# Key sums in one transfer a unit, powers per four units, Sign for ternary weights, half the key squares on GpSimd, and a new order at the end of the feed-forward

## The reference

```python
x = x + tanh(g_xattn[0]) * L0_xattn(ctx, layernorm(x))   # state-space block over ctx, gated by silu of the norm
x = x + tanh(g_ffn[0])   * L0_ffn(layernorm(x))          # gated feed-forward, weights made ternary, activations to 8 bits
x = x + tanh(g_xattn[1]) * L1_xattn(layernorm(x), ctx)   # attention, 16 heads of 128, RMS norm on q and k
x = x + tanh(g_ffn[1])   * L1_ffn(layernorm(x))          # four experts, token i goes to expert i % 4
...
gamma_w = clip(mean(abs(w)), 1e-05)
w_dq = clip(round(w / gamma_w), -1, 1) * gamma_w         # so a weight is -1, 0 or 1 times gamma_w
...
k = rmsnorm((ctx @ Wk).reshape(B, Skv, H, D), gk)        # k * (mean(k*k) + eps) ** -0.5 * gk
```

## Time and profile before

| what | value |
|---|---|
| median of 3 runs (lowest, highest) | 1853.01 us (1847.89, 1858.5) |
| the profiled execution's own time | 1852.26 us |
| its span in the profile | 1850.5 us |
| busy: PE, DVE, ACT, POOL | 1763.2, 1300.1, 963.8, 666.5 us |
| granted TensorE clock, mean | 0.983 of full speed |
| first attention step on PE | at 385.93 us |

### The profile page before, as it was taken

One profiled execution on the slowest core, in us unless ns is written; L12 is line 12 of the kernel. 1 busy time (PEld: TensorE's weight loads), 2 busy tenths in 40 slices (PEclk: granted clock), 3 DMA queues, 4 the chain that ended last, 5 costly groups with the idle time before them and its releaser, 6 DMA issues.

```text
span 1850.5 us, 19507 instructions
## 1 busy us (share of the span) xinstructions
PE 1763.2 (95%) x6114; PEld 809.9 (44%) x6114; DVE 1300.1 (70%) x1899; ACT 963.8 (52%) x1920; POOL 666.5 (36%) x696
## 2 busy tenths in 40 slices
PE   8999899879999999999999999999999899999999
PEld 4333344334444444444444444444444344445543
DVE  4989686989998689899787998987652444422221
ACT  7988786446545546566455566555435334320100
POOL 2434322337463324557222564562223333310000
PEclk9999899979999999999999999999999999999999
DMA  7999833767851146897212589732112799837110
GB/s 262 242 289 286 244 109 116 203 164 187 199 142 57 51 100 162 208 240 200 66 30 74 156 188 251 199 95 69 35 57 91 218 282 293 236 119 273 40 51 28
DMA packets 159045, 292.11 MB, mean 158 GB/s; under 512 B 18424, under 2 KB 51704, under 8 KB 156000
## 3 DMA queue, kind: packets, MB, share of 16 engines
q1 hardware_dynamic: 141664, 227.95, 39.0%
q0 software_dynamic: 17280, 62.92, 17.5%
HBM read 169.51 MB, written 58.26 MB: 123 GB/s over the span
## 4 chain that ended last, share of the span: by engine, by line
PE 72%; DVE 13%; ACT 6%; issue 4%; DMA 3%; POOL 1%; SPq 1%; DVEq 0%; ACTq 0%; POOLq 0%
PE p L846 11%; PE p L806 10%; PE p L823 9%; PE p L857 8%; PE p L893 6%; PE p L697 5%; DVE s_M L1025 5%; PE p L780 4%; PE p L829 4%; PE p L908 3%; PE p L746 3%; PE p L785 3%; DVE s_M L1020 2%; DVE s_M L1032 1%; DVE s_U L1178 1%
## 5 line engine op out<-in xcount | busy, mean ns | idle before, releaser
L1025 DVE TENSOR_TENSOR_SCAN s_M<-s_M 128x1024 f32<-128x1024 f32 x128 | 296.4, 2315 | 9.9 <-ACT s_M L1290 7.6
L1178 DVE CUSTOM_DVE_ANT_0 s_U<-p,s_U 128x512 f32<-128x512 f32 x256 | 188.2, 745 | 161.0 <-PE p L823 159.7
L823 PE MATMUL p<-s_U 128*128 128x512 f32 x512 | 268.2, 612 | 4.6 <-DVE s_U L1178 3.0
L806 PE MATMUL p<-s_U 128*128 128x512 f32 x512 | 256.7, 610 | 3.4 <-ACT s_U L1418 2.7
L1534 POOL DMA_DIRECT2D s_u<-s_M x120 | 111.7, 931 | 383.7 <-DVE s_M L1032 355.6
L1579 POOL TENSOR_SCALAR s_U<-s_U 128x512 f32<-128x512 f32 x256 | 231.9, 926 | 6.3
L857 PE MATMUL p<-s_U 128*128 128x512 f32 x512 | 223.7, 593 | 0.0
L846 PE MATMUL p<-s_U 128*128 128x512 f32 x472 | 216.0, 599 | 2.5 <-ACT s_U L1431 2.4
L1431 ACT COPY s_U<-p 128x512 f32<-128x512 f32 x196 | 105.5, 594 | 176.3 <-PE p L829 175.0
L1290 ACT ACTIVATE s_M<-s_dl,s_small 128x511 f32<-128x511 f32 x256 | 170.3, 717 | 35.5 <-DVE s_M L1025 35.3
L1426 ACT ACTIVATE s_U<-s_U 128x512 f32<-128x512 f32 x256 | 181.6, 710 | 5.3
(11 more groups left out here) (194 smaller groups left out, 2458.3 us busy)
## 6 DMA issues: line engine op xcount, KB each, us to landing
s_u<-s_M POOLq DMA_DIRECT2D x120, 512.0 KB, 7.6
s_bc<-bc_scratch SPq DMA_DIRECT2D x96, 256.0 KB, 4.5
k_scratch<-s_U SPq DMA_DIRECT2D x16, 1024.0 KB, 7.9
v_scratch<-s_U SPq DMA_DIRECT2D x16, 1024.0 KB, 5.4
s_U<-in_Wq SPq DMA_DIRECT2D x64, 256.0 KB, 6.6
s_U<-k_scratch SPq DMA_DIRECT2D x64, 256.0 KB, 5.4
s_U<-rk_scratch SPq DMA_DIRECT2D x64, 256.0 KB, 5.8
s_U<-in_Wo SPq DMA_DIRECT2D x64, 256.0 KB, 4.5
```

The costliest lines, as they stand in the source:

```text
L806: ins = e.matmul(banks[bk][:], wqq[j % 2][:, k, :], axT[b % 2][:, k, :], start=(k == 0), stop=(k == 3))
L823: e.matmul(banks[bk][:], qT[j % 3][:, k * 128:(k + 1) * 128], kT[j % 2], start=True, stop=True).then_inc(S["a_s"], 1)
L1025: e.tensor_tensor_scan(w, dA[i % 2], w, 0.0, ALU.mult, ALU.add).then_inc(S["m_s"], 1)
L1178: e.tensor_tensor_reduce(out=Pm[j % 2][:, k, :], in0=banks[ABANK[kind, j, k]][:], in1=rkb[j % 2], scale=rq[:, k:k + 1], scalar=-3.0e38, op ...
```

## The change

1. **Key sums.** `nv` writes to one of two tiles `ksr[n % 2]`. `r` is one transfer of four rows of 2 KB to a new scratch `rs_scratch`. After the second key product of the next group of four units, `ld` waits for all four and loads 128 x 64 numbers to `krs`; four `pw` of 16 columns follow after that unit's key products, and one `st` stores 128 x 64 numbers in the next unit. `rk_scratch` is laid out by group, so the first heads of the attention wait for the first group alone. The store of the keys and the load of `Wk` are issued one and two steps earlier (at `k` 3), `r` ahead of `v` 3.
2. **Key squares.** Products 0 and 2 of a unit are squared by POOL from the copy in SBUF (new instruction, a `tensor_tensor` of 128x512), 1 and 3 by ACT as before. `n` waits for both engines. The PSUM bank of an even product is given back after its copy.
3. **Ternary weights.** `clip` is gone: `put` is `Sign(x - MAGIC)` on ACT, with a bias tile `down` that POOL sets.
4. **End of the feed-forward.** In `ffn_order()` the steps `l` of a tile stand at other places among the products of the next, and `st`, `hn`, `xt` are steps of F: those of tiles 0 to 2 stand before the last residual, those of tile 3 after it. The separate list `XT` is gone.
5. The planner's tables follow, so the order changes on all engines.

```diff
-        QUANT += [("clip", w, c)] if c < 4 else []
...
-            order += [("m", t, 2 * c)] + (leave[:1] if c == 0 else []) + [("m", t, 2 * c + 1)] + (leave[3:] if c == 2 else leave[c + 1:c + 2] if c < 2 else [])
-            if c:
-                order += enter[:1]
-                enter = enter[1:]
-        order += enter
+            order += [("m", t, 2 * c)] + (leave[:1], leave[1:3], leave[3:4], enter[2:])[c]
+            order += (enter[:1] if c == 1 else []) + [("m", t, 2 * c + 1)] + (leave[4:] + enter[1:2] if c == 2 else [])
         leave = [("l", t, k) for k in range(5)]
-    return order + leave
+    order += leave[:1] + [("st", t, 0) for t in range(3)] + leave[1:4] + [("hn", t, 0) for t in range(3)] + [("xt", t, 0) for t in range(3)]
+    return order + leave[4:] + [("st", 3, 0), ("hn", 3, 0), ("xt", 3, 0)]
...
+        first, second = q > 0 and b == 0, q > 0 and b == 1
+        KV += [(b, q, "k", 0), (b, q, "k", 1)] + ([(NB - 1, q - 1, "ld", 0)] if first else []) + [(b, q, "k", 2), (b, q, "k", 3)]
+        KV += [(NB - 1, q - 1, "pw", i) for i in range(4)] if first else []
+        KV += [(b, q, "v", 0), (b, q, "v", 1), (b, q, "n", 0)] + ([(NB - 1, q - 1, "st", 0)] if second else [])
+        KV += [(b, q, "v", 2), (b, q, "nv", 0), (b, q, "r", 0), (b, q, "v", 3)]
+KV += [(NB - 1, 3, "ld", 0)] + [(NB - 1, 3, "pw", i) for i in range(4)] + [(NB - 1, 3, "st", 0)]
...
-                        e.wait_ge(S["k_sq"], 4 * n + 4)
+                        e.wait_ge(S["k_sq"], 2 * n + 2)
+                        e.wait_ge(S["k_sp"], 2 * n + 2)
...
-                        e.activation(dst, stg[c], ACT.Copy, bias=-MAGIC, saturate=False).then_inc(S["q_put"], 1)
+                        e.activation(dst, stg[c], ACT.Sign, bias=down[:], saturate=False).then_inc(S["q_put"], 1)
...
-                        e.activation(ksq[i], banks[bk][:], ACT.Square).then_inc(S["k_sq"], 1)
+                        if i % 2:
+                            e.activation(ksq[i], banks[bk][:], ACT.Square).then_inc(S["k_sq"], 1)
...
-                        if n:
-                            e.wait_ge(S["d_ksr"], 64 * n)
-                        e.activation(ksr, banks[bk][:], ACT.Copy, bias=EPS, scale=1.0 / HD).then_inc(S["k_nv"], 1)
+                        elif n:
+                            e.wait_ge(S[f"d_ksr{n % 2}"], 16 * (n // 2))
+                        e.activation(ksr[n % 2], banks[bk][:], ACT.Copy, bias=EPS, scale=1.0 / HD).then_inc(S["k_nv"], 1)
...
+                        e.tensor_tensor(ksq[i], ks[2 * n % NKS][:, i, :], ks[2 * n % NKS][:, i, :], ALU.mult).then_inc(S["k_sp"], 1)
+                    elif kind == "pw":
+                        power(krs[:, 64 * q + 16 * i:64 * q + 16 * i + 16], (S["d_kr"], 16 * (q + 1)), "k_p")
...
+                        e.dma_start(rsd[16 * q + 4 * b:16 * q + 4 * b + 4], ksr[n % 2][0:128:32, :]).then_inc(S[f"d_ksr{n % 2}"], 16)
+                    elif kind == "ld":
+                        e.wait_ge(S["d_ksr0"], 32 * (q + 1))
+                        e.wait_ge(S["d_ksr1"], 32 * (q + 1))
+                        e.dma_start(krs[:, 64 * q:64 * q + 64], rsd[16 * q:16 * q + 16].rearrange("r (p c) -> (r p) c", c=64)).then_inc(S["d_kr"], 16)
                     elif kind == "st":
-                        e.wait_ge(S["k_p"], n + 1)
-                        e.dma_start(rkd[j:j + 4].rearrange("h (p c) -> (h p) c", c=16), krs[:, 16 * n:16 * n + 16]).then_inc(S["d_rk"], 16)
+                        e.wait_ge(S["k_p"], 4 * (q + 1))
+                        e.dma_start(rkd[16 * q:16 * q + 16].rearrange("r (p c) -> (r p) c", c=64), krs[:, 64 * q:64 * q + 64]).then_inc(S["d_rk"], 16)
```

More of the change, by code:

```diff
@@ L112, in silu @@
     return b == 0 and t < 2
-XT = [("st", t) for t in range(4)] + [("hn", t) for t in range(4)] + [("xt", t) for t in range(4)]
 LBANK = {}
@@ L132 @@
             names += [("o", t)]
-    names += [("xt", t) for t in range(4)]
+        elif kind == "xt":
+            names += [("xt", t)]
     for i, x in enumerate(names):
@@ L139 @@
     for b in range(NB):
-        last = ((b - 1) % NB, q - (b == 0))
-        KV += [(b, q, "k", i) for i in range(4)] + [(b, q, "v", 0), (b, q, "v", 1), (b, q, "n", 0), (b, q, "v", 2), (b, q, "nv", 0)]
-        KV += [(*last, "pw", 0)] if q or b else []
-        KV += [(b, q, "v", 3), (b, q, "r", 0)] + ([(*last, "st", 0)] if q or b else [])
-KV += [(NB - 1, 3, "pw", 0), (NB - 1, 3, "st", 0)]
+        first, second = q > 0 and b == 0, q > 0 and b == 1
[4 more added lines that the diff above has]
+KV += [(NB - 1, 3, "ld", 0)] + [(NB - 1, 3, "pw", i) for i in range(4)] + [(NB - 1, 3, "st", 0)]
 KBANK = {}
@@ L299, in forward @@
             part(name, [("POOL", 1.3)], ("e", t, 1))
+        elif kind == "st":
+            part(("xst", t), [("DVE", 1.0), ("POOL", 1.0)], ("l", t, 4))
+        elif kind == "hn":
+            part(("xhn", t), [("DVE", 0.6)], ("xst", t), ("l", 3, 0))
+        elif kind == "xt":
+            part(("xxt", t), [("PE", 0.6), ("ACT", 0.7)], ("xhn", t), *([(NB, "q", NH * (b - 1) - 1, 3)] if b > 1 else []), take=[("xt", t)], free=[("xt", t)])
         elif k == 0:
@@ L308, in forward @@
             part(name, [("DVE", 0.8)], ("l", t, 3), ("o", t, 0), free=[("o", t)])
-    for kind, t in XT:
-        if kind == "st":
-            part(("xst", t), [("DVE", 1.0), ("POOL", 1.0)], ("l", t, 4))
-        elif kind == "hn":
-            part(("xhn", t), [("DVE", 0.6)], ("xst", t))
-        else:
-            part(("xxt", t), [("PE", 0.6), ("ACT", 0.7)], ("xhn", t), *([(NB, "q", NH * (b - 1) - 1, 3)] if b > 1 else []), take=[("xt", t)], free=[("xt", t)])
     return out
@@ L328, in weights @@
             out.append(("Q", [("ACT", 2.0)], [(0, "thr", w, 0)], (0, kind, w, c), [], []))
-        elif kind == "clip":
-            out.append(("Q", [("DVE", 1.3)], [(0, "rnd", w, c)], (0, kind, w, c), [], []))
         elif kind == "put":
-            out.append(("Q", [("ACT", 2.0)], [(0, "clip", w, c)], (0, kind, w, c), [], []))
+            out.append(("Q", [("ACT", 2.0)], [(0, "rnd", w, c)], (0, kind, w, c), [], []))
         else:
@@ L344, in keys @@
         does = {"k": [("PE", 1.75), ("ACT", 1.2)], "v": [("PE", 1.75), ("ACT", 0.6)], "n": [("PE", 1.2)], "nv": [("ACT", 0.6)],
-                "r": [("DMA", 5.0)], "pw": [("POOL", 3.0)], "st": [("DMA", 8.0 if (b, q) == (NB - 1, 3) else 2.5)]}[kind]
-        needs = {"nv": [("K", at.get((b, q, "n", 0)))], "n": [("K", at.get((b, q, "k", 3)))], "r": [("K", at.get((b, q, "nv", 0))), ("K", n - 1)], "pw": [("K", at.get((b, q, "r", 0))), ("K", n - 1)], "st": [("K", at.get((b, q, "pw", 0))), ("K", n - 1)]}.get(kind, [])
+                "r": [("DMA", 2.0)], "ld": [("DMA", 3.0)], "pw": [("POOL", 4.0)], "st": [("DMA", 8.0 if q == 3 else 2.5)]}[kind]
+        if kind == "k" and i % 2 == 0:
+            does = [("PE", 1.75), ("ACT", 0.6), ("POOL", 1.5)]
+        needs = {"nv": [("K", at.get((b, q, "n", 0)))], "n": [("K", at.get((b, q, "k", 3)))], "r": [("K", at.get((b, q, "nv", 0))), ("K", n - 1)], "ld": [("K", at.get((b, q, "r", 0))), ("K", n - 1)], "pw": [("K", at.get((b, q, "ld", 0)))], "st": [("K", at.get((b, q, "pw", 3))), ("K", n - 1)]}.get(kind, [])
         take = [bank] if kind in "kvn" else []
@@ L541, in flamingo @@
         ks = [U[:, 15360 + 2048 * i:17408 + 2048 * i].rearrange("p (h t) -> p h t", h=4) for i in range(NKS)]
-        ksr = U[:, 26624:27136]
+        ksr = [U[:, o:o + 512] for o in (26624, 25600)]
         ksq = [U[:, 21504 + 512 * i:22016 + 512 * i] for i in range(4)]
```

102 lines of the change are left out of this document (44 added, 58 removed).

## The result

The changed kernel takes **1891.9 us** (median of 4 runs, 1885.8 to 1897.5) against 1852.0 of the kernel before (4 runs on the same chip): a ratio of **1.0217, 95% interval 1.0194 to 1.024**. So it is slower beyond the noise; whether by 2% or more, the interval leaves open. The prediction was 1842 us with a range up to 1863. The profiled execution, 1897.5 us, was the longest of the four, so the two traces lie 45 us apart where the medians lie 40.

A forecast was written before the change was run, and what follows sets the result against it. The prediction took PE's work to bound the kernel, leaving only its idle and low-clock time to gain. Its terms, -9 - 11 - 4 - 2 + 8 + 3 + 2 + 5 - 2 = -10 us, gave 1842 us, range 1823 to 1863.

The forecast's parts named there:

- POOL's line: At three group borders, column sums wait for squares on POOL behind its powers and transfers: +8, +3, +2 us.
- the key sums: Before 245 us, two tiles and one transfer remove PE's 6.6 us wait and its low clock: -9 us (-3 to -9.6).
- the clips: Twelve clips, 14.6 us, leave DVE in M0; no PE wait names them, so 0 on PE.
- what lies behind the first step: After the attention's start, DVE further in M1 and new ends of F1 to F3: -2 us (-10 to +5).
- The prediction's own sign of being wrong: PE's idle time up to the attention stays at 36 us or grows, or the gain is lost between 386 and 600 us.
- End of F0, -11 and -4: Ready K work fills PE's 12.8 us idle at F0's end: -11 us; less low clock behind those waits: -4 us.
- Squares, -2: ACT loses 32 squares up to the attention, shortening PE's other waits for `nv`: -2 us (0 to -4.2).
- Rival D: Little changes: full DMA queues set the pace up to 245 us, attention starts cold; about 1850 us, chance 0.13.
- Start of the attention, +5: First attention step waits for `Wq`, loaded after the last sums, and for POOL's key power: +5 us (0 to +13).
- Rival B: Slower: PE waits for squares behind powers at borders and attention's start; 1860 us, 1871 at the extreme; chance 0.17.
- Rival C: Slower by DVE: some 22 squares on POOL hold M0's scans through the shared port lock; 1857 us, chance 0.05.

The follow-up runs named there:

- part 1 alone: Kernel before with only the key-sum change: one transfer a unit, two tiles, load and four powers every fourth unit; squares on ACT; 1863.8 us, ratio 1.0080.
- part 1 with spread powers: Kernel before with the key-sum change, but one power in each of the next four units; squares on ACT, clips kept; 1868.6 us, ratio 1.0095.
- p_tail: Kernel before with only the new order at the end of the feed-forward; 1852.5 us, ratio 1.0020.
- a_sqact: Changed kernel in its own order, but all four squares of a unit on ACT; 1870.5 us, ratio 1.0114.
- a_start: Changed kernel with Wq of the first two heads in own rooms, loaded earlier, and last sums transfer ahead of the key loads; 1889.2 us, ratio 1.0210.

## Why the prediction was wrong, step by step

The step that failed is the adding: each gain was read from one wait of one trace and taken as won, and each added cost was priced only at the places I had looked at. The terms that broke the sum are POOL's line (+13, measured 19 to 21), the key sums (-9, part 1 alone +15), the clips (0, alone +9) and what lies behind the first step (-2, +18 in the trace). The prediction's own sign of being wrong came true: PE idles 57.7 us up to the attention, where 36 or more was to refute it.

- **Key sums, -9.** The mechanism was right and the size near: two tiles gain 5 to 7. But I set nothing against it for the rest of the part, which costs some 20, so that the part alone costs 15. I read the new order of SP and took the wait for `Wk` as it stood. It vanished (7.9 us), and 9.1 us for `Wv` came, which stands in no term. The waits for `nv` were not shortened in sum: the 6.6 us went and as much came in shorter ones.
- **End of F0, -11 and -4.** The idle time was filled as described, 12.8 us fell to 1.4. The first `q` still ran 27 us later, not 4 to 14 earlier, since 19.1, 9.1 and 9.3 us of new waits stand ahead of it. No run takes part 4 out of the whole, so what it gives there is not shown: beside part 1 with spread powers it gives 9, alone it costs 4. In `p_tail`, whose order has no K there, `xt` waits 11.9 us, the first `q` is 4 us earlier even so, and the loss lies behind it (PE idles 60.5 us for 51.6).
- **Squares, -2.** In place of a relief of ACT they bring 19 us alone; it is the cost of POOL's line below, seen once more. PE's waits for `nv` stayed at 10.9 us.
- **Clips, 0.** Measured alone: +9. "No PE wait names them" was true, and the wrong question. Rival D had the full queues, but not that an engine which waits less could fill them worse, which is the likely cause and not a shown one.
- **POOL's line, +8, +3, +2.** The mechanism was right. The first border came out at 8.2 us for 8, by luck: from the fifth unit's third key product (its end at about 105.0, half way through a record of 3.60 us that starts at 103.22) POOL needed 37.8 us, with 7.85 of stand for the load that the sum left out, where +8 stands for 30; and PE needed 29.7 for 22, 5.47 of them a wait for `Wv`. The second, with a stand of 7.8 us for the load and the end of M0 ahead of the squares, cost 10.9, beyond its bound of 10. The third cost nothing. The sum also left out the low clock behind each added wait, up to 3 us each time. By `a_sqact` the squares are worth 21 us, for 13 in the sum.
- **Start of the attention, +5.** The waits were 9.3 us for `Wq` and 7.1 for POOL, beyond the bound of 13 together, but `a_start` shows that taking the first away gives 3 us at most.
- **Behind it, -2.** Measured in the trace: +18, 11.7 idle and 6.6 at a lower clock. The 7.1 us for POOL just named are part of it: the hundredth PE instruction behind the first `q` comes 8.8 us later than before (50.5 us for 41.7), the 2500th still 8.8 and the 4990th 18. So half is the attention's start, and half comes late, in waits of which none is over 4 us. No run puts that half down to a part.

Rival B named the place and the sign, and gave the extreme, 1871; the time went past it by 21 us, of which the clips' 9 were in none of its terms. Rival C was held to be excluded by rows 9, and is half right. Its scans did not stay at 2.29 us: six of the 32 of M0 took 2.9 to 4.4 us (with none above 2.5 before), the mean over all four passes went from 2315 to 2387 ns, 128 x 0.072 = 9 us on DVE, and back to 2315 in `a_sqact`. What these 9 us cost PE was not separated from PE's waits for the squares.

## What to carry to other kernels

In an order that is fixed ahead, an engine's idle share is no room. Before work is moved to it, read in the new order what stands ahead of the moved step, what each of those waits for, and who now waits at the end; a step that waits for a transfer must not stand ahead of one that the bound engine needs. Try each part alone, and take the gain (here two tiles, 0.3%) without what came with it. And work removed from an engine can make the program slower, as the twelve clips show: put the instruction back to see whether it is the removal that costs. Last, don't take an early milestone for a gain; follow the bound engine past it.
